# Turning x1 in 32x32 blocks on VectorE with transfers within SBUF, in place of TensorE's transposes

## The chip, the cores and the metric

The kernel runs on one core of one Trainium2 chip. The metric is device time in microseconds (us) of one launch. The kernel before takes 1109.47 us, the median of three runs between 1108.98 and 1109.59.

## The reference

Two layers work on x of shape (2, 1024, 256): two batches of 1024 tokens of 256 numbers. The first is a mixture of eight experts and a shared one, each of hidden size 1024. The second is a small attention pooling. All numbers are float32.

```python
g, u = einsum('bsd,edf->ebsf', h, Wg), einsum('bsd,edf->ebsf', h, Wu)
expert_outs = einsum('ebsf,efd->ebsd', silu(g) * u, Wd)
x1 = x + (1 - sg) * einsum('be,ebsd->bsd', gating_probs, expert_outs) + sg * shared   # layer 1

scores = tanh(x1 @ W1 + b1) @ v                            # one number per token
p = softmax(where(mask[prompt_type], scores, -1e30))       # (b, j, l); before, after or all but j
x2 = x1 + einsum('bjl,bld->bjd', p, x1) / cnt              # layer 2
```

## The kernel before

TensorE computes layer 1 with features on the partitions and tokens along the free dimension, so its result lies in SBUF as `xT[P, b, k, S]`: k counts the two halves of D, S the 1024 tokens. The 9 experts with 8 tiles of 128 hidden units each make 72 steps for each batch. The first pass (i = 0 to 71, batch 0) rounds the weights, uses them and keeps them in device memory. The second pass (i = NU = 72 to 143, batch 1) fetches them again. A step has seven products of a 2x2-block scheme that saves the eighth, and the sums of the down projection beside them. Each product is three matmuls (L1581, L1582, L1583) of a high and a low part in fp32r, 128x512 each.

Nothing is scheduled by a planner: each engine's program is written out by hand, and semaphores hold them together. In the second pass VectorE's `even` and `odd` alternate with i; each pair of steps is numbered p. An even step begins with `second_gate` and `second_up` (L1230, L1235), whose sums the silu and the hidden products need; an odd step ends with `rest_c("a22")` and `rest_c("a12")` (L1290). GpSimd works on SBUF beside them. SyncE's queue fetches one step's gate and up weights with `wq<-wq_kept` (L539) when product 3 of the step three before is done, and every second step a pair's down weights (`fetch_d`, L530); there are three weight slots.

Layer 2 needs x1 with tokens on the partitions, `x1[b]` of shape [P, NJ, XA]: eight blocks of 128 tokens, 256 features and two columns of ones. TensorE makes it from `xT` with transposes through the identity: `transpose_x1` (L1750) writes sixteen 128x128 blocks a batch into four PSUM banks, and ScalarE's `copy_x1` (L977) takes each bank to SBUF.

Layer 2 of batch 0 lies inside the second pass: `L1_STEP` gives it eight slots k = 0 to 7 at i = NU + 32 + 2k. Transposes stand at k = 2, 3 and 4 on TensorE, twice behind product 5 (`first_bank`) and twice behind products 7 and 6 of the next step (`second_bank`). Layer 2 of batch 1, and the pooling of both, is the tail, behind the last matmul of layer 1:

- `attn(1)` (L1698), tanh on ScalarE, `score_cols` (L1708), the copy of the scores (L959), `score_rows`, and then VectorE's chain of maxima over blocks up to `negl`.
- `block_sums(b)` (L1759) sums x1 over each block with weights `e_diag`, eight matmuls for eight blocks. ScalarE copies the sum (L987), VectorE makes its rest (`rest_sum`, L1419). This sum is what blocks give to others.
- `pool_probs` (L1777) and `pool_carries` (L1785) make the pooled rows of two blocks in one of two pairs of banks, `finish` on VectorE (L1428, L1431, L1434) divides and adds x1, and SyncE stores each pair (L547). A bank is free again when `out_done` says so.
- `pick_maxima` (L1728) spreads batch 1's maxima; `exp_carry` on ScalarE (L999) and `prob_args` on VectorE (L1401) follow it.

Where the work stands in these programs is seen in the functions below.

Of the kernel before, what the change touches and what calls it, by code (L numbers as in the profile page):

```python
# [32 lines left out]
def cond_resid_kernel(nc, x, fside, shared_gate, prompt_type, Wg, Wu, Wd, Sg, Su, Sd, W1, b1, v, out):  # L33
# [49 lines left out]
    with ExitStack() as ctx:  # L83
# [33 lines left out]
        cursor[0] += 27 * BANK * 4  # L117

        wd = sb("wd", [P, DR, 2, DN, P], F32R)
        wq_at = cursor[0]  # L120
# [102 lines left out]
        for b in range(B):  # L223
            at = l1_at[b]
            probT.append(place(f"probT{b}", [P, NJ, P], F32, at))
            at += S * 4

            neg_max.append(place(f"neg_max{b}", [2 * LANE, NJ, P], F32R, at))
            carry_r.append(place(f"carry_r{b}", [P, S], F32R, at))
            at += S * 4  # L230
            e_diag.append(place(f"e_diag{b}", [P, NJ, P], F32, at))
            at += S * 4
            attnT.append(place(f"attnT{b}", [P, BANK], F32, at))
# [11 lines left out]
            assert at + NJ * XA * 4 <= l1_at[b] + 5 * S * 4 + (NJ * XA * 4 + 511) // 512 * 512 + S * 4  # L245


        pick = place("pick", [2 * LANE, NJ, P], F32R, wq_at)
        x2 = place("x2", [P, B, NJ, D], F32, wq_at + NJ * P * 4)
# [74 lines left out]
        tanh_done = sem("tanh_done")  # L324
        x1_done = sem("x1_done")
        x1_copied = sem("x1_copied")
        x1_ones = sem("x1_ones")
        col_done = sem("col_done")
        col_ready = sem("col_ready")
# [48 lines left out]
        X1 = [[e_ps, g_ps, g_ps, e_ps], [g_ps, v_ps[1], g_ps, e_ps]]  # L378
        COL = e_ps[:, 0:NJ]
# [98 lines left out]
        def _(sp):  # L478
# [65 lines left out]
            for b in range(B):  # L544
# [284 lines left out]
        def _(act):  # L829
# [122 lines left out]
            def tanh(b):  # L952
                act.wait_ge(attn_done, b + 1)
                nc.scalar.activation(attnT[b][:], ATT[b][:], ACT.Tanh, bias=b1_sb[:, 0:1]).then_inc(tanh_done, 1)

# [12 lines left out]
            def copy_max(n):  # L968
# [3 lines left out]
                                     ACT.Copy).then_inc(max_copied, 1)  # L972

            def copy_x1(b, *banks):
                for n in banks:
                    act.wait_ge(x1_done, b * NB + n + 1)
                    nc.scalar.activation(x1[b][:, n * JB:(n + 1) * JB, 0:D],  # L977
                                         X1[b][n][:].rearrange("p (j d) -> p j d", d=D),
                                         ACT.Copy).then_inc(x1_copied, 1)

# [36 lines left out]
            def first_bank(k):  # L1017
# [3 lines left out]
                elif k == 1:  # L1021
                    copy_col(0)
                elif k == 2:
                    copy_x1(0, 0)
                elif k == 4:
                    copy_x1(0, 3)
                elif k in (6, 7):
                    copy_max(k - 6)

            def second_bank(k):  # L1030

                if k == 1:
                    copy_row(0)
                elif k in (2, 3):
                    copy_x1(0, k - 1)

# [107 lines left out]
        def _(dve):  # L1144
# [260 lines left out]
            def block_weights(b):  # L1405
# [7 lines left out]
                    ALU.mult))  # L1413

            def rest_sum(b):

# [87 lines left out]
            def odd(i, p):  # L1504
# [8 lines left out]
                rest_c("a22", p)  # L1513
                rest_c("a12", p)

            def last_odd(i, p):
# [28 lines left out]
            add_acc(0, NG - 1)  # L1545
            add_acc(1, NG - 1)
            block_weights(0)
            block_maxima(1)
# [15 lines left out]
        def _(pe):  # L1564
# [173 lines left out]

            def transpose_x1(b, *banks):
                for n in banks:  # L1740
                    if b == 0 and n >= 2:
                        pe.wait_ge(x1_copied, n - 1)
                    elif n == 2:
                        pe.wait_ge(x1_copied, NB + 1)
                    elif n == 3:
                        pe.wait_ge(col_ready, B)
                    for j in range(JB):
                        for k in range(KD):
                            tok = (n * JB + j) * P
                            mm = nc.tensor.transpose(X1[b][n][:, j * D + k * P:j * D + (k + 1) * P],  # L1750
                                                     xT[:, b, k, tok:tok + P], ident[:])
                    mm.then_inc(x1_done, 1)

            def block_sums(b, blocks):
                pe.wait_ge(dve_l1, DVE_L1["ediag", b])
                pe.wait_ge(x1_copied, NB * (b + 1))
                pe.wait_ge(x1_ones, b + 1)
                for j in blocks:
# [5 lines left out]
            def pool_probs(b, blocks):  # L1764
                for j in blocks:
                    n = b * NJ + j
                    if n == 2:

                        pe.wait_ge(sum_copied, 1)
                    elif n == 3:  # L1770
                        pe.wait_ge(x1_copied, NB + 2)
                    elif n >= len(POOLED):
                        pe.wait_ge(out_done, n - len(POOLED) + 1)
                    pe.wait_ge(x1_copied, b * NB + j * P * NB // S + 1)
                    pe.wait_ge(x1_ones, b + 1)
                    pe.wait_ge(prob_done, n + 1)
# [3 lines left out]
            def pool_carries(b, blocks):  # L1780
                pe.wait_ge(sum_copied, b + 1)
                for j in blocks:
# [7 lines left out]
                          1: ((col_ready, 1), (row_copied, 2)),  # L1790
                          2: ((x1_copied, 1), (x1_copied, 2)),
                          3: ((dve_l1, DVE_L1["earg", 0]), (x1_copied, 3)),
                          4: ((x1_copied, 4), None),
                          6: ((dve_l1, DVE_L1["parg0", 0]), None),
# [3 lines left out]
            def first_bank(k):  # L1798
# [5 lines left out]
                elif k == 1:  # L1804
                    score_cols(0)
                elif k == 2:
                    transpose_x1(0, 0)
                elif k == 3:
                    spread_blocks(0)
                elif k == 4:  # L1810
                    transpose_x1(0, 3)
                elif k in (6, 7):
                    spread_maxima(0, k - 6)

            def second_bank(k):

                if k in (1, 2, 3):
                    pe.wait_ge(silu0_done, L1_AT + L1_EVERY * k + 2)
                if k == 1:
                    score_rows(0)  # L1820
                elif k in (2, 3):
                    transpose_x1(0, k - 1)

# [46 lines left out]
            attn(1)  # L1870
            transpose_x1(1, 0, 1)
            score_cols(1)
# [3 lines left out]
            spread_blocks(1)  # L1876
            transpose_x1(1, 2, 3)
            pool_probs(0, range(2))
# [7 lines left out]
            pick_maxima(1)  # L1886
            block_sums(1, range(3))
            pool_probs(0, range(4, 6))
            pool_carries(0, range(4, 6))
            block_sums(1, range(3, NJ))  # L1890
            pool_probs(0, range(6, NJ))
            pool_carries(0, range(6, NJ))
            for j in range(0, NJ, HEAD):
                pool_probs(1, range(j, j + HEAD))
# [22 lines left out]
```

## Time and profile before

| | |
|---|---|
| median of 3 runs | 1109.47 us |
| profiled execution, its own time | 1109.52 us |
| its span, first to last instruction | 1107.8 us |
| TensorE busy | 1099.4 us (99%) |
| VectorE busy | 945.7 us (85%) |
| ScalarE busy | 745.6 us (67%) |
| GpSimd busy | 605.8 us (55%) |
| mean granted TensorE clock | 0.999 of full speed |

The profile is one execution, so its numbers are compared with its own 1109.52 us. PE is TensorE, DVE VectorE, ACT ScalarE, POOL GpSimd and SP SyncE; SPq and ACTq are their DMA issues, which the busy times leave out. A DMA row in order of time gives how long the issuing took, not the transfer; the time to landing stands in a view of its own. A row with "x2" and a time merges two that lie close, so its time runs from the start of the first to the end of the last. Tile names in rows leave out numbers: `a` and `s` are the hidden sums, `x` is x1 or x2, `acc_of`, `v_both`, `g_ps` and `e_ps` are PSUM banks.

### The profile page before, as it was taken

What the parts mean: (1) busy time and instruction counts of PE and PEld (TensorE: products, weight loads), DVE (VectorE), ACT (ScalarE), POOL (GpSimd) and SP (SyncE); (2) the same over time, 40 slices, a digit from 0 to 9 for tenths busy, and PEclk for the clock granted to TensorE, in tenths of its full rate; (3) what the DMA queues carried; (4) which work ended last, traced back from release to release, by engine and by line L of the source; (5) the groups of instructions that cost most, each with busy time, mean ns of one, the idle gap of its engine ahead of it and who ended that gap; (6) DMA issues with size and microseconds to landing.
All of it is one profiled execution on the core that took longest, in us unless ns stands there. A gap on an engine that the chain in (4) does not pass through costs nothing.

```text
span 1107.8 us, 15953 instructions
## 1 busy us (share of the span) xinstructions
PE 1099.4 (99%) x4840; PEld 901.4 (81%) x4840; DVE 945.7 (85%) x1223; ACT 745.6 (67%) x1335; POOL 605.8 (55%) x524
## 2 busy tenths in 40 slices
PE   8999999999999999999999999999999999999998
PEld 5888888888888888888888888888788888888876
DVE  7878889888888888888689888888789988888885
ACT  6776777677677676766666666666566666666673
POOL 7666666656666666565436565654343444444441
PEclk9999999999999999999999999999999999999999
DMA  6785676676667666666765555565455555555512
GB/s 225 212 282 227 254 265 229 252 261 229 238 256 261 227 258 250 231 245 239 300 236 207 196 196 206 209 209 209 176 180 177 200 209 209 209 202 198 198 68 77
DMA packets 73716, 241.24 MB, mean 218 GB/s; under 512 B 14752, under 2 KB 45984, under 8 KB 64416
## 3 DMA queue, kind: packets, MB, share of 16 engines
q1 hardware_dynamic: 72816, 239.70, 59.9%
q8 instruction: 40, 0.66, 0.2%
q10 hardware_dynamic: 816, 0.52, 0.2%
q14 instruction: 44, 0.36, 0.1%
HBM read 134.29 MB, written 105.91 MB: 217 GB/s over the span
## 4 chain that ended last, share of the span: by engine, by line
PE 93%; POOL 3%; DVE 1%; issue 1%; DMA 0%; ACT 0%; ACTq 0%; DVEq 0%; POOLq 0%
PE acc_of L1581 11%; PE acc_of L1583 11%; PE acc_of L1582 11%; PE v_both L1581 9%; PE v_both L1583 8%; PE v_both L1582 8%; PE g_ps L1581 6%; PE e_ps L1581 6%; PE e_ps L1583 6%; PE e_ps L1582 6%; PE g_ps L1582 6%; PE g_ps L1583 6%; DVE a_lo L1290 0%; DMA raw<-in_L_cond_Wg 0%; POOL mask_part L691 0%
## 5 line engine op out<-in xcount | busy, mean ns | idle before, releaser
L896 ACT ACTIVATE silu<-g_ps 128x512 f32<-128x512 f32 x144 | 86.3, 599 | 173.5 <-PE g_ps L1583 173.3
L1581 PE MATMUL v_both<-xs_hi,wq 128*128 128x512 f32 x432 | 168.6, 390 | 0.6 <-DVE xs_lo L1181 0.5
L1583 PE MATMUL v_both<-xs_lo,wq 128*128 128x512 f32 x432 | 168.2, 389 | 0.0
L1582 PE MATMUL v_both<-xs_hi,wq 128*128 128x512 f32 x432 | 168.1, 389 | 0.0
L1235 DVE TENSOR_TENSOR up<-v_both,p_sb 128x512 f32<-128x512 f32 x144 | 99.4, 690 | 47.6 <-PE v_both L1583 43.6
L761 POOL TENSOR_TENSOR a<-a,a_own 128x512 f32<-128x512 f32 x35 | 56.1, 1604 | 133.6 <-DVE a_own L1262 133.6
L1230 DVE TENSOR_TENSOR gate<-e_ps,v_part 128x512 f32<-128x512 f32 x144 | 98.8, 686 | 33.4 <-PE e_ps L1583 32.6
L902 ACT ACTIVATE p_sb<-e_ps 128x512 f32<-128x512 f32 x144 | 86.2, 599 | 52.2 <-PE e_ps L1583 51.8
L1192 DVE TENSOR_TENSOR wq<-raw,wq 128x896 fp32r<-128x896 f32 (+1 forms) x70 | 119.8, 1711 | 0.0
L1581 PE MATMUL g_ps<-xs_hi,wq 128*128 128x512 f32 x288 | 113.0, 392 | 1.0 <-ACT v_both L890 0.4
L1581 PE MATMUL e_ps<-xs_hi,wq 128*128 128x512 f32 x288 | 112.5, 391 | 1.3 <-ACT p_sb L902 1.1
L890 ACT ACTIVATE v_both<-g_ps 128x512 f32<-128x512 f32 x144 | 84.5, 587 | 41.8 <-PE g_ps L1583 39.8
L1583 PE MATMUL g_ps<-xs_lo,wq 128*128 128x512 f32 x288 | 112.1, 389 | 0.0
L1582 PE MATMUL g_ps<-xs_hi,wq 128*128 128x512 f32 x288 | 112.1, 389 | 0.0
L1582 PE MATMUL e_ps<-xs_hi,wq 128*128 128x512 f32 x288 | 112.1, 389 | 0.0
L1583 PE MATMUL e_ps<-xs_lo,wq 128*128 128x512 f32 x288 | 112.1, 389 | 0.0
L1581 PE MATMUL acc_of<-h_hi,wd 128*128 128x512 f32 x288 | 112.0, 389 | 0.0
L1582 PE MATMUL acc_of<-h_hi,wd 128*128 128x512 f32 x288 | 112.0, 389 | 0.0
L1583 PE MATMUL acc_of<-h_lo,wd 128*128 128x512 f32 x288 | 112.0, 389 | 0.0
L758 POOL TENSOR_TENSOR s<-a_own,a 128x512 f32<-128x512 f32 x35 | 54.7, 1563 | 96.6 <-DVE a_own L1281 94.8
L600 POOL TENSOR_TENSOR wd<-raw_d,wd 128x512 fp32r<-128x512 f32 x35 | 45.4, 1296 | 106.6 <-ACT wd L872 106.6
L1290 DVE TENSOR_TENSOR a_lo<-a_own,a_hi 128x512 fp32r<-128x512 f32 x72 | 84.8, 1178 | 14.5 <-ACT a_hi L950 14.5
(268 smaller groups left out, 2866.1 us busy)
## 6 DMA issues: line engine op xcount, KB each, us to landing
wq_kept<-wq SPq DMA_DIRECT2D x72, 896.0 KB, 4.5
wq<-wq_kept SPq DMA_DIRECT2D x72, 896.0 KB, 4.5
wd_kept<-wd SPq DMA_DIRECT2D x36, 1024.0 KB, 6.5
wd<-wd_kept SPq DMA_DIRECT2D x36, 1024.0 KB, 6.0
raw_d<-in_L_cond_Wd SPq DMA_DIRECT2D x32, 256.0 KB, 4.5
raw<-in_L_cond_Wg SPq DMA_DIRECT2D x31, 256.0 KB, 2.6
raw<-in_L_cond_Wu SPq DMA_DIRECT2D x31, 256.0 KB, 3.2
out_x<-x SPq DMA_DIRECT2D x8, 256.0 KB, 2.1
```

The costliest lines, as they stand in the source:

```text
L758: nc.gpsimd.tensor_tensor(s3[:], a_own[:], a21[p % 2][:], ALU.subtract).then_inc(sum_made["s3"], 1)
L761: nc.gpsimd.tensor_tensor(a21[p % 2][:], a21[p % 2][:], a_own[:], ALU.add).then_inc(sum_made["s1"], 1)
L890: nc.scalar.activation(v_ps[i % 2][:], g_ps[:], ACT.Copy).then_inc(seeded, 1)
L896: nc.scalar.activation(silu0[:, i % 2, :], g_ps[:], ACT.Silu).then_inc(silu0_done, 1)
L902: nc.scalar.activation(p7_sb[:], e_ps[:], ACT.Copy).then_inc(p7_copied, 1)
L1192: nc.vector.tensor_tensor(lo[:, part, :], raw[:, s, 1 + part.start:8, j * P:(j + 1) * P], hi[:, part, :].bitcast(F32), ALU.subtract).then_ ...
L1230: nc.vector.tensor_tensor(gate1[:], e_ps[:], v_part[:], ALU.add).then_inc(gate1_done, 1)
L1235: nc.vector.tensor_tensor(up1[:], v_ps[i % 2][:], p7_sb[:], ALU.add).then_inc(up1_done, 1)
L1290: nc.vector.tensor_tensor(lo, src[:], hi.bitcast(F32), ALU.subtract).then_inc(c_split[q], 1)
L1581: nc.tensor.matmul(ps, w_hi, a_hi, start=start, stop=False, skip_group_check=True)
L1582: nc.tensor.matmul(ps, w_lo, a_hi, start=False, stop=False, skip_group_check=True)
L1583: return nc.tensor.matmul(ps, w_hi, a_lo, start=False, stop=stop, skip_group_check=True)
```

## The change

TensorE's 32 transposes and ScalarE's eight copies go. In their place, for each batch:

- VectorE turns `xT` into `x1_cut[b]` with four instructions (`turn_x1`), each of 128x512: it transposes every 32x32 block within its place. For batch 0 they stand at the ends of the odd steps NU+9, NU+11, NU+13 and NU+15, for batch 1 between the last additions to `xT` and `block_weights(0)`.
- 32 DMAs (`move_x1`) put the blocks to their partitions, from SBUF to SBUF, each from 32 partitions to 32 partitions, 32 KB in 256 pieces of 128 bytes. For batch 0 SyncE issues four behind the weight fetch of each of the second pass's steps n = 17 to 24, once all four `turn_x1` are done. For batch 1 SyncE issues 20 and ScalarE 12.
- TensorE's `block_sums` and `pool_probs` wait for all 32 DMAs of their batch (`x1_ready`), where they waited for a copied bank. In batch 0, `tanh(0)` waits for them as well, since `attnT0` and what follows it lie where `x1_cut0` was.
- `block_sums(1)` is split 4 + 4 instead of 3 + 5, and both parts stand one pair of pooled blocks of batch 0 later.

```diff
+        TURN_X1_0 = {NU + 9 + 2 * (k * NT + t): (k, t) for k in range(KD) for t in range(NT)}
+        MOVE_X1 = {17 + n: range(4 * n, 4 * n + 4) for n in range(8)}
+        MOVED_BY_SP = 20
+        MOVES = list(itertools.product(range(KD), range(P // CUT), range(P // CUT)))
+
+        def move_x1(queue, b, n):
+            k, a, c = MOVES[n]
+            cols = slice(k * P + a * CUT, k * P + (a + 1) * CUT)
+            queue.dma_start(x1[b][c * CUT:(c + 1) * CUT, :, cols], x1_cut[b][a * CUT:(a + 1) * CUT, k, c, :, :]
+                            ).then_inc(x1_moved[b], 16)
...
@@ SyncE, second pass
                 if n % PAIR == 0 and n:
                     fetch_d(n // PAIR - 1)
+                if n in MOVE_X1:
+                    sp.wait_ge(x1_turned[0], KD * NT)
+                    for m in MOVE_X1[n]:
+                        move_x1(sp, 0, m)
             fetch_d(SPS)
+            sp.wait_ge(x1_turned[1], KD * NT)
+            sp.wait_ge(p_done[3], NG)
+            for n in range(0, MOVED_BY_SP):
+                move_x1(sp, 1, n)
...
@@ ScalarE, tail
             tanh(1)
-            copy_x1(1, 0)
+            act.wait_ge(x1_turned[1], KD * NT)
+            act.wait_ge(p_done[3], NG)
+            acts = iter(range(MOVED_BY_SP, len(MOVES)))
+            for n in itertools.islice(acts, 2):
+                move_x1(act, 1, n)
             copy_col(1)
+            for n in itertools.islice(acts, 1):
+                move_x1(act, 1, n)
             copy_row(1)
-            copy_x1(1, 1)
+            for n in itertools.islice(acts, 3):
+                move_x1(act, 1, n)
             copy_sum(0)
-            copy_x1(1, 2, 3)
+            for n in itertools.islice(acts, 3):
+                move_x1(act, 1, n)
             exp_blocks(1)
+            for n in acts:
+                move_x1(act, 1, n)
...
@@ VectorE
+            def turn_x1(b, k, t):
+                tok = slice(t * BANK, (t + 1) * BANK)
+                dve.wait_ge(acc_read[t], KD * (b + 1))
+                nc.vector.transpose(x1_cut[b][:, k, :, t * NJ // NT:(t + 1) * NJ // NT, :].rearrange("p c j d -> p j c d"),
+                                    xT[:, b, k, tok].rearrange("p (j c d) -> p j c d", c=P // CUT, d=CUT)
+                                    ).then_inc(x1_turned[b], 1)
...
@@ TensorE
-            def transpose_x1(b, *banks):
...
+            def x1_ready(b):
+                pe.wait_ge(x1_moved[b], len(MOVES) * 16)
+                pe.wait_ge(x1_ones, b + 1)
```

On TensorE the tail is written in another order. From the block maxima (L1719) to the end of batch 1's block sums, the program before reads as follows (`x_0` is x1 of batch 0, `x_1` of batch 1; `neg_r,pick` is `pick_maxima`):

```order
L1719 MATMUL acc_of<-blk_max_diag,ones 128x8
L1750 MATMUL g_ps<-ident,xT 128x128 x4
L1750 MATMUL e_ps<-ident,xT 128x128 x4
L1777 MATMUL acc_of<-x_0_170,probT_158 128x258 x2
L1785 MATMUL acc_of<-blk_sum,carry_r_160 128x258 x2
L1777 MATMUL v_both<-x_0_170,probT_158 128x258 x2
L1785 MATMUL v_both<-blk_sum,carry_r_160 128x258 x2
L1728 MATMUL acc_of<-neg_r_182,pick 128x128 x8
L1759 MATMUL g_ps<-x_1_183,e_diag_174 128x258 x3
L1777 MATMUL acc_of<-x_0_170,probT_158 128x258 x2
L1785 MATMUL acc_of<-blk_sum,carry_r_160 128x258 x2
L1759 MATMUL g_ps<-x_1_183,e_diag_174 128x258 x5
```

The same place of the changed program:

```order
L1758 MATMUL acc_of<-blk_max_diag,ones 128x8
L1801 MATMUL acc_of<-x_0_171,probT_158 128x258 x2
L1809 MATMUL acc_of<-blk_sum,carry_r_160 128x258 x2
L1801 MATMUL v_both<-x_0_171,probT_158 128x258 x2
L1809 MATMUL v_both<-blk_sum,carry_r_160 128x258 x2
L1767 MATMUL acc_of<-neg_r_183,pick 128x128 x8
L1801 MATMUL acc_of<-x_0_171,probT_158 128x258 x2
L1809 MATMUL acc_of<-blk_sum,carry_r_160 128x258 x2
L1786 MATMUL g_ps<-x_1_184,e_diag_175 128x258 x4
L1801 MATMUL v_both<-x_0_171,probT_158 128x258 x2
L1809 MATMUL v_both<-blk_sum,carry_r_160 128x258 x2
L1786 MATMUL g_ps<-x_1_184,e_diag_175 128x258 x4
```

The transposes between the block maxima and the pooling are gone, the pair of blocks 4 and 5 comes ahead of batch 1's first block sums, and the pair 6 and 7 ahead of the last.

SyncE's queue, from the weight fetch of step n = 17 of the second pass to that of n = 19, now holds the moves of batch 0 (`x_0<-x_cut`); what a row waits for stands in brackets:

```order
L557 DMA wq<-wq_kept 128x1792 [waits p3_done,wq_stored0]
L477 DMA x_0_171<-x_cut_162 32x8x32 [waits x1_turned0]
L477 DMA x_0_171<-x_cut_162 32x8x32 x3
L557 DMA wq<-wq_kept 128x1792 [waits p3_done,wq_stored1]
L548 DMA wd<-wd_kept 128x2048 [waits s4_used]
L477 DMA x_0_171<-x_cut_162 32x8x32 [waits x1_turned0]
L477 DMA x_0_171<-x_cut_162 32x8x32 x3
L557 DMA wq<-wq_kept 128x1792 [waits p3_done,wq_stored2]
```

Before, the fetches of n = 17, 18 and 19 followed one another with only the down weights between them. Now the fetch of n = 18 stands behind the wait for VectorE's fourth `turn_x1`, and behind four issues.

## Rows read from the trace of the kernel before

**Rows 1.** The page: busy time by engine, and the chain by engine.

```profile
PE 1099.4 (99%) x4840; PEld 901.4 (81%) x4840; DVE 945.7 (85%) x1223; ACT 745.6 (67%) x1335; POOL 605.8 (55%) x524
PE 93%; POOL 3%; DVE 1%; issue 1%; DMA 0%; ACT 0%; ACTq 0%; DVEq 0%; POOLq 0%
```

**Rows 2.** Stretch: start:end, us, busy us (x instructions) each, clock, DMA, GB/s.

```profile
640.00:700.00 60.00, 59.93 (x265) 49.27 (x264) 53.20 (x73) 38.33 (x70) 38.42 (x39) 1.00 0.55 199
```

**Rows 3.** Chain of waits, step NU+36: start us, us, engine, tile, line.

```profile
815.69 0.44 PE e_ps L1750 x4
```

**Rows 4.** VectorE in order of time: start us, us, line, operation, out<-in.

```profile
111.08 0.70 DVE L1175 STREAM_TRANSPOSE xT<-x_cut 128x512 f32<-128x512 f32 x1
```

**Rows 5.** VectorE and TensorE in order of time, steps NU+14 and NU+15.

```profile
653.26 0.69 DVE L1235 TENSOR_TENSOR up<-v_both,p_sb 128x512 f32<-128x512 f32 x1
655.10 0.39 PE L1581 MATMUL v_both<-xs_hi,wq 128*128 128x512 f32 x1
665.00 1.74 DVE L1290 TENSOR_TENSOR a_lo<-a,a_hi 128x512 fp32r<-128x512 f32 x1
```

**Rows 6.** SyncE and TensorE in order of time; the landing (page).

```profile
656.02 7.50 SPq L539 DMA_DIRECT2D wq<-wq_kept  x2
673.87 0.39 PE L1581 MATMUL g_ps<-xs_hi,wq 128*128 128x512 f32 x1
wq<-wq_kept SPq DMA_DIRECT2D x72, 896.0 KB, 4.5
```

**Rows 7.** DMA issues in order of time, kernel's start: SyncE and ScalarE.

```profile
0.81 1.46 SPq L469 DMA_DIRECT2D x_nat<-in_x  x3
33.91 1.63 SPq L475 DMA_DIRECT2D x_cut<-in_x  x2
1.35 0.49 ACTq L454 DMA_DIRECT2D raw<-in_L_cond_Wg  x1
```

**Rows 8.** DMA issues: tiles, queue, count, KB each, median us from issue to landing.

```profile
out_x<-x SPq DMA_DIRECT2D x8, 256.0 KB, 2.1
x_cut<-in_x SPq DMA_DIRECT2D x8, 128.0 KB, 5.0
```

**Rows 9.** DMA from 47 to 49 us: packets, and share of 16 engines.

```profile
DMA packets 1916, 0.25 MB, mean 124 GB/s; under 512 B 1915, under 2 KB 1915, under 8 KB 1916
q1 hardware_dynamic: 1916, 0.25, 78.1%
```

**Rows 10.** Chain of waits, the tail, in order of time.

```profile
1089.09 0.58 PE g_ps L1750 x4
1089.68 0.44 PE e_ps L1750 x4
1092.34 1.04 PE acc_of L1728 x8
1095.98 2.18 PE g_ps L1759 x10
1098.16 0.87 PE v_both L1777 x4
1099.31 0.17 DVE den L1428
```

**Rows 11.** The tail in order of time: VectorE and ScalarE.

```profile
1080.00 0.68 DVE L1318 TENSOR_TENSOR xT<-e_ps,xT 128x512 f32<-128x512 f32 x1
1083.28 0.69 ACT L954 ACTIVATE attnT<-acc_of,b_sb 128x512 f32<-128x512 f32 x1 [2.77 <-PE acc_of L1698]
1085.11 0.20 ACT L959 ACTIVATE score_col<-e_ps 128x32 f32<-128x32 f32 x1 [0.66 <-PE e_ps L1708]
1093.02 2.18 ACT L999 ACTIVATE carry<-acc_of,carry_bias 128x128 f32<-128x128 f32 x8 [2.12 <-PE acc_of L1728]
1096.30 0.88 DVE L1434 SCALAR_TENSOR_TENSOR x<-v_both,rden,x 128x256 f32<-128x256 f32 x2
1098.62 0.42 DVE L1419 TENSOR_TENSOR blk_sum<-g_ps,blk_sum 32x258 fp32r<-32x258 f32 x1 [0.27 <-ACT blk_sum L987]
```

More of the change, by code:

```diff
@@ L1 @@
+import itertools
 from contextlib import ExitStack
@@ L117, in cond_resid_kernel @@
         cursor[0] += 27 * BANK * 4
+        wd_at = cursor[0]
         wd = sb("wd", [P, DR, 2, DN, P], F32R)
@@ L232, in cond_resid_kernel @@
             at += S * 4
+            if b == 0:
+                x1_cut = [place("x1_cut0", [P, KD, P // CUT, NJ, CUT], F32, at)]
+                assert at + S * KD * 4 <= l1_at[1]
             attnT.append(place(f"attnT{b}", [P, BANK], F32, at))
@@ L245, in cond_resid_kernel @@
             assert at + NJ * XA * 4 <= l1_at[b] + 5 * S * 4 + (NJ * XA * 4 + 511) // 512 * 512 + S * 4
+        x1_cut.append(place("x1_cut1", [P, KD, P // CUT, NJ, CUT], F32, wd_at + 2 * DN * P * 4))
         pick = place("pick", [2 * LANE, NJ, P], F32R, wq_at)
@@ L324, in cond_resid_kernel @@
         tanh_done = sem("tanh_done")
-        x1_done = sem("x1_done")
-        x1_copied = sem("x1_copied")
         x1_ones = sem("x1_ones")
+        x1_turned = [sem(f"x1_turned{b}") for b in range(B)]
+        x1_moved = [sem(f"x1_moved{b}") for b in range(B)]
         col_done = sem("col_done")
@@ L377, in cond_resid_kernel @@
         L1_STEP = {L1_AT + L1_EVERY * k: k for k in range(8)}
-        X1 = [[e_ps, g_ps, g_ps, e_ps], [g_ps, v_ps[1], g_ps, e_ps]]
         COL = e_ps[:, 0:NJ]
@@ L953, in tanh @@
                 act.wait_ge(attn_done, b + 1)
+                if b == 0:
+                    act.wait_ge(x1_moved[0], len(MOVES) * 16)
                 nc.scalar.activation(attnT[b][:], ATT[b][:], ACT.Tanh, bias=b1_sb[:, 0:1]).then_inc(tanh_done, 1)
@@ L972, in copy_max @@
                                      ACT.Copy).then_inc(max_copied, 1)
[L974 to L979, printed above, removed]
             def exp_blocks(b):
@@ L1022, in first_bank @@
                     copy_col(0)
[L1023 to L1026, printed above, removed]
                 elif k in (6, 7):
@@ L1033, in second_bank @@
                     copy_row(0)
-                elif k in (2, 3):
-                    copy_x1(0, k - 1)
             round_x(0, 1)
@@ L1514, in odd @@
                 rest_c("a12", p)
+                if i in TURN_X1_0:
+                    turn_x1(0, *TURN_X1_0[i])
             def last_odd(i, p):
@@ L1546, in _ @@
             add_acc(1, NG - 1)
+            for k in range(KD):
+                for t in range(NT):
+                    turn_x1(1, k, t)
             block_weights(0)
@@ L1737, in spread_maxima @@
                                  start=True, stop=True).then_inc(max_done, 1)
-            def transpose_x1(b, *banks):
[L1740 to L1752, printed above, removed]
+            def x1_ready(b):
+                pe.wait_ge(x1_moved[b], len(MOVES) * 16)
+                pe.wait_ge(x1_ones, b + 1)
             def block_sums(b, blocks):
                 pe.wait_ge(dve_l1, DVE_L1["ediag", b])
-                pe.wait_ge(x1_copied, NB * (b + 1))
-                pe.wait_ge(x1_ones, b + 1)
+                x1_ready(b)
                 for j in blocks:
@@ L1769, in pool_probs @@
                         pe.wait_ge(sum_copied, 1)
-                    elif n == 3:
-                        pe.wait_ge(x1_copied, NB + 2)
                     elif n >= len(POOLED):
                         pe.wait_ge(out_done, n - len(POOLED) + 1)
-                    pe.wait_ge(x1_copied, b * NB + j * P * NB // S + 1)
-                    pe.wait_ge(x1_ones, b + 1)
+                    x1_ready(b)
                     pe.wait_ge(prob_done, n + 1)
@@ L1790, in _ @@
                           1: ((col_ready, 1), (row_copied, 2)),
-                          2: ((x1_copied, 1), (x1_copied, 2)),
-                          3: ((dve_l1, DVE_L1["earg", 0]), (x1_copied, 3)),
-                          4: ((x1_copied, 4), None),
+                          3: ((dve_l1, DVE_L1["earg", 0]), None),
                           6: ((dve_l1, DVE_L1["parg0", 0]), None),
@@ L1805, in first_bank @@
                     score_cols(0)
-                elif k == 2:
-                    transpose_x1(0, 0)
                 elif k == 3:
                     spread_blocks(0)
-                elif k == 4:
-                    transpose_x1(0, 3)
                 elif k in (6, 7):
@@ L1815, in second_bank @@
             def second_bank(k):
-                if k in (1, 2, 3):
+                if k == 1:
                     pe.wait_ge(silu0_done, L1_AT + L1_EVERY * k + 2)
-                if k == 1:
                     score_rows(0)
-                elif k in (2, 3):
-                    transpose_x1(0, k - 1)
             pe.wait_ge(blank_ready, 1)
@@ L1870, in _ @@
             attn(1)
-            transpose_x1(1, 0, 1)
             score_cols(1)
@@ L1876, in _ @@
             spread_blocks(1)
-            transpose_x1(1, 2, 3)
             pool_probs(0, range(2))
@@ L1886, in _ @@
             pick_maxima(1)
-            block_sums(1, range(3))
             pool_probs(0, range(4, 6))
             pool_carries(0, range(4, 6))
-            block_sums(1, range(3, NJ))
+            block_sums(1, range(4))
             pool_probs(0, range(6, NJ))
             pool_carries(0, range(6, NJ))
+            block_sums(1, range(4, NJ))
             for j in range(0, NJ, HEAD):
```

## The prediction

> **What bounds the kernel now.** I read the page first, for the engine that sets the time. TensorE is busy for 1099.4 of 1107.8 us and has 93% of the chain [rows 1]. The stretches say whether that holds where batch 0's part of the change lies: from 640 to 700 us TensorE is busy for 59.93 of 60 us, and VectorE for 53.20 [rows 2]. So there an instruction less on TensorE is worth its whole place, and one more on VectorE costs nothing while it stays within some 6.8 us of slack in 60. Then I read the chain in the tail, where no engine is full: it alternates between TensorE and VectorE, and its last 8.5 us, from 1099.31 to 1107.8, are five rounds of `finish` on VectorE and the last store [rows 10]. In the tail it matters when VectorE can begin these five rounds, and nothing else.
>
> **Batch 0: what goes.** In step NU+36 four transposes hold the chain for 0.44 us [rows 3]. Batch 0 has four such places, all in the full stretch, so 4 x 0.44 = 1.76 us go. The four ScalarE copies go too, at no gain: ScalarE is busy for 38.33 of 60 us [rows 2].
>
> **Batch 0: what comes, on VectorE.** A transposing instruction of 128x512 took 0.70 us in the first pass [rows 4]. Each of the four new ones pushes the next even step's `second_gate` and `second_up` back by that much. In step NU+14, after an odd step that is to carry one, `up` ended at 653.95 and TensorE took product 3, which waits for it, at 655.10 [rows 5]: 1.15 us to spare, so 0.70 fits and I take nothing. The new ones write a strided target and share SBUF with GpSimd; a subtraction of the same size beside GpSimd took 1.74 us [rows 5]. At that price each would miss by 0.6 us, 2.4 us for four; below nothing it can't go. Without this cover the cost is what exceeds 1.15 us, four times.
>
> **Batch 0: what comes, on SyncE's queue.** Behind the fetch of n = 17, at 656.02, SyncE waits for the fourth `turn_x1` at the end of step NU+15. That step's last subtraction ended at 666.74 [rows 5], so the turning ends at 667.4. Four issues follow. Three x_nat issues of 256 pieces each took 1.46 us, 0.49 each [rows 7], so four take 2.0, and the fetch of n = 18 is issued at 669.4. Before, it was issued at 656.02 + 7.50 - 0.32 = 663.2. It lands 4.5 us later [rows 6], at 673.9. TensorE needs these weights for product 1 of n = 18, which stands within the step before and began at 673.87 [rows 6]. So a slack of 6.2 us is used up to the last tenth. I take a stall of 0.3 us, for four small transfers that run ahead of it; bounds are 0 and 1.4, the latter with a turning of 1.74 us. The next fetch is delayed by the four issues only, and has a step of 7.1 us to recover. Data is no bound: 1916 packets of 128 bytes took 78.1% of 2 us [rows 9], so 8192 take 6.7 us of all engines, spread over eight steps whose DMA share is 0.55 [rows 2].
>
> **Batch 1: what goes.** Transposes 0 and 1 stood under ScalarE's tanh, which ran from 1083.28 to 1083.97 [rows 11]; they gave nothing to the end. Transposes 2 and 3 stood on the chain, 0.58 + 0.44 = 1.02 us [rows 10], ahead of the pooling. Without them `pick_maxima` starts at 1091.3 instead of 1092.34, and after it (1.04 us) and the pooling of blocks 4 and 5 (0.87 + 0.28, as for 6 and 7) [rows 10] TensorE stands before `block_sums(1)` at 1093.5.
>
> **Batch 1: what comes.** When is x1 of batch 1 complete? The last addition to `xT` ends at 1080.68 [rows 11]; four turnings of 0.70 make it 1083.5. SyncE then issues 20 transfers at 0.49 each, so the last begins 19 x 0.49 = 9.3 us later, at 1092.8. A transfer of 256 pieces from SBUF landed 2.1 us after its issue [rows 8]: 1094.9. ScalarE's twelve issues cost the same each, by its own row of 0.49 [rows 7]. Two fit between tanh and the score copy at 1085.11 [rows 11], the others between its later copies and `exp`, and the last is out before SyncE's. They delay none of its work by more than 0.3 us; `carry`, which started at 1093.02 waiting for `pick_maxima` [rows 11], becomes up to 1.0 us earlier, and I take 0.5.
>
> So TensorE, ready at 1093.5, waits until 1094.9. From there: eight blocks of sums at 2.18 / 5 = 0.44 us are 3.5, the pair 6 and 7 between them 1.15, then ScalarE's copy and VectorE's rest, 0.88 us from 1098.16 to the end of the row at 1098.62 [rows 10, 11]. That is 5.5, with 0.1 to restart TensorE 5.6: VectorE begins its five rounds at 1100.5 instead of 1099.31, 1.2 us later. In the old order the pair 6 and 7 ran behind the sums and hid the copy and the rest; in the new one these stand open, so the later place of the sums costs some of what it saves.
>
> There is a floor under that. The pair 6 and 7 needs the banks of 2 and 3, free at 1097.18 [rows 11] less the 0.5 above, 1096.7. Then 0.44 and 0.28 for block 7, 1.75 for four sums and 0.88 give 1100.0, or 0.7 us later than before, however early the transfers land (0.2 to 1.2 for 1.0 and 0 in place of 0.5). The transfers decide from a landing at 1100.0 - 5.6 = 1094.4 on.
>
> **The sum.** -1.76 + 0.3 + 1.2 = -0.3 us, against the profiled execution's 1109.52, which is 0.05 above the median: 1109.2 us. About 0.2%, 2.2 us, is what a measurement of this kernel can tell from no change; this is far within.
>
> **The price of one issue** carries the most. A lone issue in the second pass took 0.32 us, the end of its row [rows 6]; at 0.37 each the last lands at 1083.5 + 7.0 + 2.1 = 1092.6, below the floor's point. Two x_cut issues with 1024 pieces of 128 bytes took 1.63 us, 0.81 each [rows 7]; at that price the last lands at 1083.5 + 15.5 + 2.1 = 1101.1. I take 0.49, the row with the same number of pieces. The landing is bounded by the same rows, 2.1 and 5.0 us [rows 8]; the 5.0 stood behind large transfers, so I take 2.1.
>
> The Trainium skill speaks against so many small transfers: DMA: Bandwidth & Descriptors, section Rules for kernel authors, has it that under 64 KB a transfer is mostly overhead and many should be coalesced into one. By that rule the issues would cost more than their bytes suggest, which is the second rival below; here the x_nat row, with 256 KB at 0.49 us an issue, shows that bytes hardly matter to the issue, and no row shows what a 32 KB one costs. The same section says that spreading transfers over the issuing engines saves only issue time. By the rows issue time (9.8 us for 20) exceeds the data's 6.7, so this is the case in which the split helps.
>
> **Rivals.**
>
> *The transfers land early.* If an issue costs 0.46 us or less, or the landing is shorter, the floor holds: -1.76 + 0.3 + 0.7 = -0.8, with 0.2 for the floor and no stall -1.6: 1107.9 to 1108.7, say 1108.5. For it speaks the lone issue of 0.32; against it that every burst at the start ran at 0.49.
>
> *The transfers land late, and the kernel is slower.* Place: TensorE before `block_sums(1)`. Each us of landing beyond 1094.4 is a us of time. It decides against the change from a landing at 1095.2 on, where the tail takes back the whole 1.5 of the steady part. At 0.65 us an issue, between the two rows, the last lands at 1083.5 + 12.4 + 2.1 = 1098.0, VectorE starts 4.3 us late, and the time is 1109.52 - 1.5 + 4.3 = 1112.3. At 0.81 it is 1109.52 - 1.5 + 7.4 = 1115.4.
>
> *The steady part stalls.* A turning beside GpSimd takes 1.74 us, TensorE waits for `up` four times (2.4) and 1.4 for the fetch of n = 18. Then 1109.52 - 1.76 + 2.4 + 1.4 + 1.2 = 1112.8; half of it gives 1110.9. Against it speak 6.8 us of idle VectorE in 60.
>
> *More is saved than I count.* With early transfers and no floor, batch 1's sums end 1.15 - 1.02 = 0.13 us later than before, and VectorE starts 0.88 us behind them instead of 1.15, so 0.1 earlier: 1109.52 - 1.76 - 0.1 = 1107.6. The freed ScalarE in the second pass could add a few tenths where TensorE waits for it now: down to 1107.1.
>
> **How the numbers follow.** The forecast 0.40, early transfers 0.27, late ones 0.18, stalls 0.08, more saved 0.07. Faster by over 0.2% (below 1107.3) needs the last case or the bottom of the second: 0.12. Slower by over 0.2% (above 1111.7) is most of the late transfers and part of the stalls, 0.22. Within: 0.66. The range reaches down to 1107.4, the bottom of the early case less a little, and up to 1112.8, past the 1112.3 of the late one; outside are issues at 0.7 us or more, and a saving beyond 2.1 us.
>
> **What would show each step.** Right: 32 matmul rows of L1750 gone with no new wait of TensorE between 600 and 700 us, save one below 0.5 us near 673 for weights; four transposing rows of about 0.7 us; moves issued every 0.5 us; TensorE idle for about a us before batch 1's block sums, which end with the first `finish` round of the last five at about 1100.5 less the steady gain. Wrong: an issue pitch of 0.4 or 0.6, landings other than 2 us, a transposing row beyond 1.15 us, or a last `den` chain that does not follow the block sums. A time below 1107.4 would mean that a wait I hold for a floor is none; one above 1112.8 that an issue costs what 1024 pieces cost.

## The result: 6.4 us slower, and the profile after

The changed kernel takes 1115.88 us, the median of four runs from 1115.50 to 1116.25; the kernel before took 1109.49 beside it (four runs, 1108.98 to 1109.59). The ratio is 1.0057, with an interval of 1.0045 to 1.0069. That is slower by 6.4 us, where the forecast was 1109.2 and the range ended at 1112.8. The profiled execution has a span of 1113.8 us against 1107.8.

The page of the changed kernel first: busy time by engine, the chain by engine, and the group of matmuls that waits for weights (busy us, mean ns | idle before it, and what ended most of it).

```profile
PE 1098.6 (99%) x4808; PEld 899.5 (81%) x4808; DVE 954.0 (86%) x1231; ACT 742.5 (67%) x1327; POOL 604.3 (54%) x524
PE 92%; POOL 3%; DVE 2%; DMA 1%; issue 1%; ACT 1%; SPq 0%; ACTq 0%; DVEq 0%; POOLq 0%
L1620 PE MATMUL g_ps<-xs_hi,wq 128*128 128x512 f32 x288 | 113.0, 392 | 2.2 <-DMA wq<-wq_kept 1.2
```

TensorE has 32 instructions less than in [rows 1] and is busy for only 0.8 us less, while the span grew by 6.0: so most of the loss is TensorE standing idle, and some is TensorE working slowly. The third row has a releaser that is new, a weight fetch.

Where the time went is seen with two marks that both kernels have: the start of `attn(1)`, which ends the steady part, and the `den` with which VectorE begins the last five `finish` rounds. Both are rows in order of time, here of the changed kernel.

```profile
1078.64 3.70 PE L1737 MATMUL acc_of<-xT,W_sb 128*128 128x512 f32 x8 [0.21 <-DVE xT L1344]
```

The same row of the kernel before stands at 1079.54, and its `den` at 1099.31 [rows 10]. So up to `attn(1)` the change gains 0.9 us. Of these 0.24 are there already at the fetch of n = 17 (655.78 instead of 656.02), ahead of the first move; over the nine traces of this case that fetch lies between 655.78 and 656.63, so some tenths of a us at these marks are the execution's and not the change's. From `attn(1)` to the `den` it takes 26.60 us instead of 19.77. Behind the `den` both take the same within 0.1 us.

**The second pass.** VectorE, SyncE and TensorE in order of time (start us, us; in brackets idle us and what ended it), where batch 0's moves begin:

```profile
651.69 0.70 DVE L1445 STREAM_TRANSPOSE x_cut<-xT 128x512 f32<-128x512 f32 x1
655.78 0.32 SPq L557 DMA_DIRECT2D wq<-wq_kept  x1
666.16 0.70 DVE L1445 STREAM_TRANSPOSE x_cut<-xT 128x512 f32<-128x512 f32 x1
666.89 2.73 SPq L477 DMA_DIRECT2D x<-x_cut  x4
669.71 0.54 SPq L557 DMA_DIRECT2D wq<-wq_kept  x1
674.70 0.50 PE L1620 MATMUL g_ps<-xs_hi,wq 128*128 128x512 f32 x1 [1.22 <-DMA wq<-wq_kept]
```

This is the place of [rows 6]. The turning ends at 666.86, earlier than the forecast 667.4, but the four issues behind it take 2.73 us, and the fetch of n = 18 is issued at 669.71. The DMA view of this one fetch has it landed after 4.9 us. Product 1 of n = 18 began at 673.87 before. Here TensorE stands at it some 0.5 us earlier, waits 1.22 us by the row's bracket, and begins it at 674.70.

**The tail.** VectorE, the two issuing queues, ScalarE and TensorE in order of time:

```profile
1079.70 2.48 DVE L1445 STREAM_TRANSPOSE x_cut<-xT 128x512 f32<-128x512 f32 x4
1082.21 13.47 SPq L477 DMA_DIRECT2D x<-x_cut  x20
1090.13 1.95 ACTq L477 DMA_DIRECT2D x<-x_cut  x3
1092.18 2.17 ACT L1021 ACTIVATE carry<-acc_of,carry_bias 128x128 f32<-128x128 f32 x8 [1.86 <-PE acc_of L1767]
1092.37 0.59 PE L1809 MATMUL acc_of<-blk_sum,carry_r 128*128 128x258 f32 x2
1097.12 3.78 PE L1786 MATMUL g_ps<-x,e_diag 128*128 128x258 f32 x8 [4.17 <-DVE rden L1465]
```

The turning is done at 1082.18, ScalarE's last issue at 1092.08, but SyncE's twentieth begins only at 1095.1: (1095.1 - 1082.21) / 19 = 0.68 us from one issue to the next. TensorE is done with blocks 4 and 5 at 1092.95 and idles for 4.17 us. The brackets name VectorE's `rden`, whose row ended at 1096.60, half a us before TensorE moved; the wait is for several semaphores, and the one that came last is that of the transfers. The DMA view gives the landing (KB each, median us from issue to landing), and 1095.1 plus 2.0 is 1097.1:

```profile
x<-x_cut SPq DMA_DIRECT2D x20, 32.0 KB, 2.0
```

ScalarE's last three issues stand right ahead of `carry`, which begins 0.10 us after they end and so 13.54 us behind `attn(1)`, where it was 13.48 before [rows 11]. The forecast had it 0.5 us earlier.

Then something that the forecast did not have at all. The same eight rows of block sums (four matmuls of the high part and four of the low) take 3.78 us here, and 1.76 in the chain below, where the other four blocks are summed. The stretches show why (columns as in [rows 2]; the clock is the column after the five busy times):

```profile
1093.00:1095.00 2.00, 0.00 (x0) 0.00 (x0) 1.24 (x2) 2.00 (x8) 0.00 (x0) 1.00 0.30 50
1095.00:1096.00 1.00, 0.00 (x0) 0.00 (x0) 0.93 (x5) 1.00 (x5) 0.99 (x1) 0.56 0.39 66
1096.00:1101.00 5.00, 3.88 (x9) 3.16 (x10) 1.43 (x5) 1.12 (x4) 1.54 (x2) 0.50 0.49 164
1101.00:1102.00 1.00, 1.00 (x5) 0.73 (x4) 0.00 (x0) 0.00 (x0) 0.00 (x0) 0.53 0.00 0
1102.00:1103.00 1.00, 1.00 (x7) 0.92 (x6) 0.00 (x0) 0.00 (x0) 0.00 (x0) 1.00 0.00 0
```

The granted clock falls to half, the 1.2 GHz level, at about 1095, when TensorE has stood idle for some 2 us, and comes back at about 1102, when it has worked for 5. What it does in between takes twice as long. The chain of waits of the changed kernel shows the path through all this (start us, us, engine, tile, line):

```profile
1096.60 0.52 issue
1097.12 3.78 PE g_ps L1786 x8
1100.90 1.45 PE v_both L1801 x4
1102.35 0.24 PE v_both L1809 x2
1102.59 1.76 PE g_ps L1786 x8
1104.37 0.40 ACT blk_sum L1009
1104.79 0.42 DVE blk_sum L1453
1105.24 0.17 DVE den L1462
```

The copy and the rest, 0.87 us from 1104.37 to 1105.24, stand open behind the last sums, as forecast. The last row answers to the `den` at 1099.31 in [rows 10].

### The profile page after: what moved, and what is told of

It reads as the page before. It is cut to its first block, busy times and chain, and to the rows that moved or that the text cites. A ratio compares the mean times of both kernels' runs of the same rounds, so it can differ in the third digit from the quotient of the medians.

```text
span 1113.8 us, 15951 instructions
## 1 busy us (share of the span) xinstructions
PE 1098.6 (99%) x4808; PEld 899.5 (81%) x4808; DVE 954.0 (86%) x1231; ACT 742.5 (67%) x1327; POOL 604.3 (54%) x524
## 4 chain that ended last, share of the span: by engine, by line
PE 92%; POOL 3%; DVE 2%; DMA 1%; issue 1%; ACT 1%; SPq 0%; ACTq 0%; DVEq 0%; POOLq 0%
PE acc_of L1620 11%; PE acc_of L1621 10%; PE acc_of L1622 10%; PE v_both L1620 8%; PE v_both L1622 8%; PE v_both L1621 8%; PE g_ps L1620 6%; PE g_ps L1622 6%; PE g_ps L1621 6%; PE e_ps L1620 6%; PE e_ps L1621 6%; PE e_ps L1622 6%; DVE a_lo L1316 1%; PE g_ps L1786 0%; DMA wq<-wq_kept 0%
## 5 line engine op out<-in xcount | busy, mean ns | idle before, releaser
L1288 DVE SCALAR_TENSOR_TENSOR h<-silu,gates,up 128x512 f32<-128x512 f32 x72 | 89.7, 1245 | 10.4 <-ACT silu L941 4.4
```

What stands on the lines that cost most here:

```text
L1288: nc.vector.scalar_tensor_tensor(out=dst[:], in0=silu1[:], scalar=gate_of(i), in1=up1[:], op0=ALU.mult, op1=ALU.mult).then_inc(h_done[1], 1)
```

## The experiments

Seven kernels were run, each beside runs of the kernel before on the same chip. e1, e2, e3 and e5 shared one chip (before: 1109.59, 27 runs), e4, e6 and e7 another (before: 1109.37, 22 runs). "Tail" is the time from the start of `attn(1)` to the `den` of the last five rounds. It and the column before it come from the one profiled execution of each kernel; that of e1 is the fastest of its eleven (1108.33) and that of e7 the fastest of its five (1112.72), so their `attn(1)` may stand some tenths of a us early.

| kernel | us (runs) | ratio, interval | attn(1) at | tail |
|---|---|---|---|---|
| before | 1109.47 | | 1079.54 | 19.77 |
| after | 1115.88 (4) | 1.0057, 1.0045 to 1.0069 | 1078.64 | 26.60 |
| e1, batch 0's part only | 1109.06 (11) | 0.9995, 0.9986 to 1.0003 | 1077.98 | 19.76 |
| e2, the same, moves two steps later | 1107.79 (11) | 0.9981, 0.9973 to 0.9990 | 1077.21 | 19.77 |
| e5, before with the later sums only | 1111.12 (11) | 1.0012, 1.0003 to 1.0021 | 1079.60 | 21.32 |
| e3, after, TensorE busy too long | 1117.11 (4) | 1.0066, 1.0052 to 1.0079 | 1079.28 | 27.54 |
| e7, after, TensorE busy in the wait | 1113.52 (5) | 1.0038, 1.0025 to 1.0051 | 1078.30 | 24.21 |
| e4, after with 16 transfers for batch 1 | 1109.47 (10) | 1.0003, 0.9994 to 1.0012 | 1078.67 | 20.48 |
| e6, e4 with both orders mended | 1107.06 (11) | 0.9979, 0.9971 to 0.9988 | 1077.45 | 19.68 |

**e1: batch 0's part alone.** The kernel before, with these edits of the change and nothing of batch 1's:

```diff
+        TURN_X1_0 = {NU + 9 + 2 * (k * NT + t): (k, t) for k in range(KD) for t in range(NT)}
+        MOVE_X1 = {17 + n: range(4 * n, 4 * n + 4) for n in range(8)}
...
-                elif k == 2:
-                    transpose_x1(0, 0)
```

> The kernel before with batch 0's part of the change alone: its 16 transposes and 4 copies go, the four turnings and 32 transfers come, batch 1 stays as it was. Theory A (late transfers and the clock in batch 1's tail make the whole loss): the four places give back 4 x 0.47 us, the fetch of n = 18 stalls TensorE once by 1.2 us as in the changed kernel, so 0.7 us faster than before, 1108.8 us. Rival B (VectorE, pushed back, or the added traffic costs in the second pass as well): at or above 1109.5 us.

1109.06 us. The tail is that of before to 0.01 us, so batch 0's part acts ahead of the tail alone. The point lies between the two expectations and the interval takes in no change; by the trace the stall for weights is 0.9 us here. What the four places are worth without it is read from the next run.

**e2: the same, with the moves behind n = 19 to 26.**

```diff
-        MOVE_X1 = {17 + n: range(4 * n, 4 * n + 4) for n in range(8)}
+        MOVE_X1 = {19 + n: range(4 * n, 4 * n + 4) for n in range(8)}
```

> As e1, but the transfers of batch 0 are issued behind the fetches of n = 19 to 26 instead of 17 to 24, when the turning is long done, so that no fetch stands behind a wait. Theory A (the stall comes from the wait for the fourth turning, ahead of the fetch of n = 18): no stall, the whole 4 x 0.47 = 1.9 us is kept, 1107.6 us, with the fetch that follows four issues 2.8 us late but on time. Rival C (the four issues of 0.68 us each are what delays a fetch too far): again a stall of about a us, 1108.8 us.

1107.79 us, 1.8 below before, with an interval that excludes 1. Its queue in order of time:

```profile
656.00 7.18 SPq L554 DMA_DIRECT2D wq<-wq_kept  x2
670.34 0.32 SPq L554 DMA_DIRECT2D wq<-wq_kept  x1
670.71 2.72 SPq L474 DMA_DIRECT2D x<-x_cut  x4
```

The issue of the fetch of n = 18 ends at 663.18 (663.52 before), because the wait for the turning now stands behind n = 19, at a time when the turning is done. Its page has no group left that waits for a weight fetch. From 656.00 to `attn(1)` it takes 421.21 us against 423.52 of before: 2.3 us gained, 0.5 more than the four places of 0.44. About 0.3 of that lies near 661 us, where TensorE's rows before start 0.46 and 0.34 us apart instead of 0.23, and in e2 hardly more than 0.23. Whether the freed ScalarE gives it, as the last rival has it, was not tested. The moves of batch 0 themselves cost nothing that shows.

**e5: the kernel before with batch 1's block sums later.** No transfer, only the new order of the tail:

```diff
-            block_sums(1, range(3))
             pool_probs(0, range(4, 6))
             pool_carries(0, range(4, 6))
-            block_sums(1, range(3, NJ))
+            block_sums(1, range(4))
             pool_probs(0, range(6, NJ))
             pool_carries(0, range(6, NJ))
+            block_sums(1, range(4, NJ))
```

> The kernel before with batch 1's block sums later alone: pooled blocks 4 and 5, then four sums, then 6 and 7, then four sums; the transposes stay on TensorE. By the steps of the prediction (the pair 6 and 7 no longer hides the copy and rest of the sum, and waits for the banks of 2 and 3) VectorE's last five rounds begin about 1.2 us later: 1110.7 us. Rival E (the order costs nothing): 1109.5 us.

1111.12 us, 1.5 slower, where 1.2 was expected. Its chain of waits:

```profile
1096.35 0.50 DVE x L1434
1096.89 1.14 PE v_both L1777 x4
1098.03 0.24 PE v_both L1785 x2
1098.27 1.76 PE g_ps L1759 x8
1100.05 0.40 ACT blk_sum L987
1100.92 0.17 DVE den L1428
```

The pair 6 and 7 waits for its bank until VectorE's `x` is done; then the last four sums, the copy and the rest follow in a row. This is the floor as the prediction described it. Here the transposes still stand on the chain ahead of it, and `carry` begins 13.47 us behind `attn(1)`. In e4 below it is 12.65, and that difference of 0.82 us is what lies between the tail's +1.55 here and the +0.71 there.

**e3 and e7: TensorE busy while it waits.** The changed kernel with matmuls of which nothing is used, into a free bank, ahead of batch 1's first sums; nine in e3, four in e7:

```diff
+            for _ in range(9):   # e7: range(4)
+                nc.tensor.matmul(g_ps[:], ident[:], xT[:, 0, 0, 0:BANK], start=True, stop=True, skip_group_check=True)
             block_sums(1, range(4))
```

> The changed kernel, with nine matmuls of 128x512 in float32 into the bank of batch 1's block sums, whose result is overwritten, at the place where TensorE waits 4.2 us for batch 1's transfers. They take 9 x 0.43 = 3.9 us. Theory A (after the wait TensorE runs at half clock, 1.2 GHz, for some 5 us, and this costs 2.6 us): the clock stays full, block sums take 0.44 us each again, 1113.3 us. Rival D (block sums are slow at first because transfers and VectorE share SBUF with them, or the extra matmuls run past the landing): 1115.9 us or more.

1117.11 us. This one missed for a reason of its own: it was sized with too short a matmul. One takes 0.88 us (two rows of 0.44), so nine ran past the landing. TensorE in order of time, kernel e3:

```profile
1093.43 7.89 PE L1903 MATMUL g_ps<-xT,ident 128*128 128x512 f32 x18
1101.15 1.91 PE L1786 MATMUL g_ps<-x,e_diag 128*128 128x258 f32 x8
```

The sums behind take 1.91 us, at a clock of 1.00, so the clock stays up when TensorE stays busy; the time says nothing on what the lower one costs. e7 has four.

> e3 again with four extra matmuls instead of nine, since one in float32 holds TensorE for 0.88 us and nine ran 3.6 us past the landing. Four take 3.5 us and end before the transfers land. Theory A (the half clock behind the wait costs 2.6 us): 1113.3 us. Rival D (the block sums were slow for another reason): 1115.9 us.

1113.52 us, 2.36 less than the changed kernel, by its tail 26.60 - 24.21 = 2.39. TensorE in order of time, and the stretches, kernel e7:

```profile
1092.45 3.60 PE L1903 MATMUL g_ps<-xT,ident 128*128 128x512 f32 x8
1096.77 1.98 PE L1786 MATMUL g_ps<-x,e_diag 128*128 128x258 f32 x8 [0.72 <-DVE rden L1465]
```

```profile
1092.00:1096.00 4.00, 4.00 (x12) 1.75 (x10) 2.50 (x7) 4.00 (x14) 1.27 (x1) 1.00 0.34 58
1096.00:1100.00 4.00, 3.28 (x17) 2.89 (x17) 1.09 (x4) 0.79 (x3) 1.26 (x1) 1.00 0.61 205
```

The sums begin when the transfers land, 0.35 us earlier than in the changed kernel, as its `attn(1)` also does (0.34); nothing else of the wait is changed. They take 1.98 us instead of 3.78, and the four rows of L1801 behind them, where the clock was still low in the changed kernel (1.45), take 0.87. So the lower clock costs 2.4 us, and the wait itself the rest.

**e4: batch 1 in 16 transfers.** Both halves of the features go in one transfer, 512 pieces of 128 bytes, SyncE issues 10 where it issued 20, and ScalarE 6 where it issued 12. For that, x1 of batch 1 lies as 16 runs of 129:

```diff
-        MOVED_BY_SP = 20
+        MOVED_BY_SP = 10
+        BOTH = list(itertools.product(range(P // CUT), range(P // CUT)))
...
+            if b:
+                a, c = BOTH[n]
+                queue.dma_start(x1[1][c * CUT:(c + 1) * CUT, :, a * CUT:(a + 1) * CUT],
+                                x1_cut[1][a * CUT:(a + 1) * CUT, c, :, :]).then_inc(x1_moved[b], 16)
+                return
```

> The changed kernel with batch 1's blocks moved by 16 transfers of 64 KB in 512 pieces of 128 bytes (both halves of D in one; x1 of batch 1 lies as 16 runs of 129 numbers, so that source and target have three dimensions) instead of 32 of 256 pieces; SyncE issues 10, ScalarE 6. Bytes, pieces and the order of TensorE are the same. Theory A (the price is per issue, 0.68 us, hardly per piece): SyncE's last issue ends 6.8 to 7.2 us after the turning, the last transfer lands 9 us after it instead of 15, TensorE's wait before batch 1's block sums and the half clock behind it vanish, and what is left is the order's 1.5 us and the stall's 1.2: 1110.5 us. Rival F (the pieces set the pace: 8192 pieces take as long however they are cut): each issue 1.3 us, landing as late as before, 1115.9 us.

1109.47 us, level with before and 6.4 below the changed kernel. SyncE and TensorE in order of time, kernel e4:

```profile
1082.23 7.28 SPq L478 DMA_DIRECT2D x<-x_cut  x10
1092.38 0.59 PE L1828 MATMUL acc_of<-blk_sum,carry_r 128*128 128x258 f32 x2
1092.81 1.90 PE L1802 MATMUL g_ps<-x,e_diag 128*128 128x258 f32 x8
1095.13 1.14 PE L1819 MATMUL v_both<-x,probT 128*128 128x258 f32 x4 [0.42 <-DVE x L1483]
```

An issue with twice the pieces takes 0.73 us instead of 0.68, so ten are out at 1089.51, 6.2 us before the twenty. The block sums follow the pair 4 and 5 without a wait, the clock stays, and what TensorE then waits for is a bank, 0.42 us. The data are the same 8192 pieces, so in the changed kernel it was the number of issues that set the landing, not the pieces. The tail is 20.48 us, 0.71 over before: the floor, which the prediction had at 0.7. The expectation's 1110.5 had taken e5's 1.5 for it.

That floor holds with ScalarE's six issues. The chain of waits of e4 has `carry` at

```profile
1091.32 0.40 ACT carry L1027 x2
```

which is 0.83 us nearer to `attn(1)` than with twelve issues in the changed kernel. The bank that TensorE waits for comes free behind `carry` and VectorE's rows, so with twelve the floor would be some 0.71 + 0.83 = 1.5 us (an estimate from these rows, not run).

**e6: e4 with the block sums at their old places and batch 0's moves from n = 19 on.**

```diff
-        MOVE_X1 = {17 + n: range(4 * n, 4 * n + 4) for n in range(8)}
+        MOVE_X1 = {19 + n: range(4 * n, 4 * n + 4) for n in range(8)}
...
+            block_sums(1, range(3))
             pool_probs(0, range(4, 6))
             pool_carries(0, range(4, 6))
-            block_sums(1, range(4))
+            block_sums(1, range(3, NJ))
             pool_probs(0, range(6, NJ))
             pool_carries(0, range(6, NJ))
-            block_sums(1, range(4, NJ))
```

> e4 with two more edits: batch 0's transfers behind the fetches of n = 19 to 26, and batch 1's block sums at the place they had before (3 ahead of the pooled blocks 4 and 5, 5 behind them). Theory A: the whole 1.9 us of the second pass, plus 0.5 to 1.0 us in the tail, because transposes 2 and 3 leave the chain and the sums of batch 1 wait little: 1106.8 us, faster than both kernels and than e2. Rival G (the transfers still land after TensorE reaches the first sums, now ahead of the pooled blocks 4 and 5): 1107.8 to 1109 us.

1107.06 us, 2.3 below before, with an interval that excludes 1: it beats both kernels, and stands level with e2, whose interval overlaps its own. Its chain of waits:

```profile
1089.41 1.03 PE acc_of L1782 x8
1090.45 0.71 issue
1091.16 1.54 PE g_ps L1802 x6
1095.98 0.87 PE v_both L1819 x4
1097.13 0.17 DVE den L1472
```

TensorE waits 0.71 us ahead of the sums. Its sequencer stands in the chain as "issue", with no releaser; the trace has only the transfers open then, the last of SyncE's issued at about 1087.6 and landed 3.5 us later. So rival G's wait is there, though the time is below its range, and it takes back most of what the absent transposes give. Even so the order that the change gave up would have been the better one, with transfers as early as these: the tail is 19.68 us, 0.1 below before, where the expectation had 0.5 to 1.0. Nearly all of the 2.3 us comes from batch 0. Batch 1's transfers, in the best form tried, give 0.1.

## Why the prediction was wrong

The forecast was 1109.2, the measured time 1115.88. The steps, in its order:

- **The four places of batch 0, -1.76: right.** The fetches of the second pass, from n = 17 to n = 71, lie 0.67 us closer in the changed kernel with a stall of 1.22, so 1.89 are gained, 0.47 a place. e2 gives 2.3 in all, of which 0.3 has another place.
- **VectorE's turning at nothing: right.** 0.70 us each in the second pass, and no row of TensorE there with a wait for `up`. The rival of a slower turning falls.
- **The fetch of n = 18, +0.3: mis-sized, 1.22.** The turning ended 0.6 us before the forecast. But the four issues took 2.73 us instead of 2.0, the fetch's own issue 0.54 instead of 0.32 and its landing 4.9 instead of 4.5, and TensorE needed the weights 0.5 us earlier. e2 takes the stall away by an order in which nothing waits ahead of a fetch.
- **Transposes 2 and 3 leave the chain, -1.02: right, a little less.** `pick_maxima` begins 11.90 us behind `attn(1)`, where it was 12.73: 0.83. TensorE was ready at 1092.95; 1093.5 less the 0.9 gained up to `attn(1)` is 1092.6.
- **The price of one issue, 0.49: this is the step that failed.** It was taken from `x_nat <- in_x` because the number of pieces was the same [rows 7]. The transfer within SBUF from 32 to 32 partitions took 0.68, above the middle of the bounds 0.37 to 0.81. The text says that every burst at the start ran at 0.49. It did not: the two x_cut issues of its own [rows 7] took 0.81 each, and the trace before has small transfers among them that cost more than the large, 0.2 KB for 0.60:

```profile
11.86 0.60 SPq L496 DMA_DIRECT2D b_sb<-in_L_cond_b  x1
12.50 0.60 SPq L497 DMA_DIRECT2D v_sb<-in_L_cond_v  x1
```

From the turning's measured end and with the measured landing, 1082.2 + 19 x 0.68 + 2.0 gives 1097.1, as measured. So the wait of TensorE and where it stands were right, and a size was off, to which the text itself gave the largest weight. That ScalarE's issues are all out first was right as well (1092.08), but not that they delay none of its work by more than 0.3: they hold `carry` back by 0.8 us against e4. Here this cost nothing, as the transfers came later still.

- **The late rival, 18%: its mechanism is what came.** By its own sum an issue of 0.68 lands the last transfer at 1083.5 + 12.9 + 2.1 = 1098.5, and the time is 1109.52 - 1.5 + 4.1 + 0.7 = 1112.8, the end of the range. So the price of an issue alone moves the forecast by 3.6 us, to the end of the range; most of what lies beyond 1112.8 is the next step's.
- **From the landing 5.6 us: missing a term, which failed as well.** From 1097.12 to the `den` it was 8.12. Of the 2.5 more, 2.4 are the lower clock, by e7. No step asked what an idle TensorE does to what follows. In the late rival each us of landing was to cost a us; with the wait as long as it came, the clock added 2.4.
- **The floor, +0.7, and the open copy and rest: right**, by e4 (+0.71), though with half of ScalarE's issues; with the twelve of the forecast it would be some 1.5 by the estimate above.

The sum from the runs, in differences of the traces: -0.90 up to `attn(1)`; +0.71 for the order (e4 less before); +3.73 for the landing (e7 less e4, 24.21 - 20.48); +2.39 for the clock (after less e7). That is +5.93, the difference of the two `den` rows (1105.24 - 1099.31); the terms are differences along one line of kernels, so they must add up to it. Of the +3.73, the wait is 4.17, less what e4 waits for a bank behind it, 0.42.

The Trainium skill has the missing term: TensorE: Matmul & The Clock Gate, section HAM oscillation — how this bites in real kernels, describes a kernel whose TensorE waits for a DMA, falls to the lower clock and starts its next work there. The trace agrees, with 3.78 us for sums that otherwise take 1.76. The Trainium skill, DMA: Bandwidth & Descriptors, section Issuing engines are not separate DMA queues, calls the time to initiate a DMA usually small beside the DMA itself. Here it is not: SyncE spent 13.47 us on issuing what lands 2.0 us after each issue, and e4, which halves the issues and keeps the bytes, takes the whole 6.4 us back.

Two things stay open. Why an issue from 32 partitions of SBUF costs 0.68 us where one from device memory with as many pieces cost 0.49 was not separated into partitions, source and place. Neighbours in a burst are a small part of it: ScalarE's single moves took 0.59 and 0.61 each. And the fall of the clock was seen in one wait only: it fell in the one of 4.17 us, and not in those of 0.72 (e7), 0.71 (e6) and 0.42 (e4). Nothing between was run.

## What to carry to other kernels

When many small transfers replace work on an engine, count the issues on each queue and time one issue of the very same shape first; twenty at 0.68 us took 13.5 us, and merging two into one nearly halved that. Count them on the engine that also computes, too: its work waits behind them. A new wait of TensorE has to be priced with the work behind it, which here ran at 1.2 GHz and cost 2.4 us on top of the wait's own. A queue's wait for one engine does not belong ahead of a fetch that another engine needs: behind it, the same four issues a step were free.

## What the hardware showed beyond that

- One issue on SyncE: 0.32 us alone for 896 KB of weights, 0.54 and 0.81 for the same right behind a burst of moves (rows below), 0.60 for 0.2 KB at the kernel's start, 0.68 for 32 KB from 32 to 32 partitions in 256 pieces, 0.73 for 64 KB in 512. Bytes hardly matter to it, and the issue next behind a burst was dearer than one alone.
- Landing of a 32 KB transfer within SBUF: 2.0 us in the tail. With 64 KB each it was 3.0 in the median and 3.5 for the last, in e4 and e6, so e6's sums waited for x1 until 1091.16. The DMA share of the stretches goes with it: 0.47 to 0.53 from 1084 to 1090 in the changed kernel, 0.99 to 1.60 in e4, where the pieces come twice as fast. The same 32 KB took 5.9 us (median of eleven) in the second pass, among the weight fetches from 664 to 676 us.
- A matmul of 128x512 in plain float32 takes 0.88 us, two rows of 0.44 in the trace.

SyncE of the changed kernel in order of time, behind the rows shown above:

```profile
670.77 2.85 SPq L477 DMA_DIRECT2D x<-x_cut  x4
673.72 0.81 SPq L557 DMA_DIRECT2D wq<-wq_kept  x1
```
